# One layer of Mamba and experts in chunks: the residual projection in two buffers, its SiLU beside the gates', the second norm turned earlier

## The reference

```python
def _forward(x, rms_w, W_in, conv_w, conv_b, W_x, W_dt, A_log, W_out):
    xn = _rmsnorm(x, rms_w)
    xs, res = jnp.split(xn @ W_in, 2, axis=-1)
    # xs = silu(causal depthwise convolution of xs with 4 taps + conv_b)
    dt, Bm, Cm = jnp.split(xs @ W_x, [D_INNER, D_INNER + D_STATE], axis=-1)
    dt = jax.nn.softplus(dt @ W_dt)
    # over the tokens: h = exp(A * dt) * h + dt * B * xs;  y = sum over the states of h * C
    y = y * jax.nn.silu(res)
    return x + y @ W_out

x = x + _forward(_layernorm(x), ...)      # x: 1 x 4096 x 256, f32
x = x + experts(_layernorm(x))            # 8 experts, 512 tokens each, width 704:
                                          # (silu(x @ w1) * (x @ w3)) @ w2
```

## Time and profile before

| | |
|---|---|
| median of 3 runs | 1064.31 us (1063.12 to 1065.66) |
| the profiled execution | 1064.04 us |
| its span, first to last instruction | 1062.2 us |
| VectorE busy | 934.8 us, 88% |
| GpSimd busy | 891.4 us, 84% |
| TensorE busy | 944.7 us, 89% |
| ScalarE busy | 698.8 us, 66% |
| mean granted clock of TensorE | 0.958 |

### The profile page before, as it was taken

How to read it: one execution, slowest core, us unless ns; L and a number is a source line. 1 busy time by engine, 2 the same in 40 slices (tenths; PEclk the granted TensorE clock), 3 DMA queues, 4 the chain that set the end, 5 groups by cost and what they waited for, 6 DMA issues and landing times.

```text
span 1062.2 us, 13010 instructions
## 1 busy us (share of the span) xinstructions
PE 944.7 (89%) x4160; PEld 598.6 (56%) x4160; DVE 934.8 (88%) x1011; ACT 698.8 (66%) x1188; POOL 891.4 (84%) x491
## 2 busy tenths in 40 slices
PE   5988789889998999989999889989999897769879
PEld 4554455555664556645665556645666455655655
DVE  5797799899998999898998999898998989998941
ACT  4665675776767766776768867676767766567520
POOL 1598799897998999897998989987998979998910
PEclk9999899999999999989999999999999999769889
DMA  5570153102821047011641029010570026200110
GB/s 162 238 283 20 42 223 134 41 23 94 301 84 62 1 177 300 1 63 55 247 177 39 23 97 356 26 62 1 207 271 6 38 95 257 88 20 6 51 48 20
DMA packets 42852, 117.86 MB, mean 111 GB/s; under 512 B 8608, under 2 KB 27040, under 8 KB 32672
## 3 DMA queue, kind: packets, MB, share of 16 engines
q1 hardware_dynamic: 40928, 116.99, 30.2%
q10 hardware_dynamic: 1856, 0.04, 0.1%
HBM read 110.21 MB, written 6.82 MB: 110 GB/s over the span
## 4 chain that ended last, share of the span: by engine, by line
PE 32%; DVE 31%; issue 15%; ACT 15%; POOL 6%; DMA 1%; DVEq 0%; POOLq 0%; ACTq 0%; SPq 0%
PE gbank L1046 21%; DVE ring L663 20%; DVE ring L648 7%; PE ybank L1109 6%; ACT ebank L801 4%; POOL hc L512 3%; POOL ring L498 2%; PE gbank L1060 2%; ACT sres L865 1%; ACT xs L861 1%; ACT xin L955 1%; ACT L866 1%; ACT hb L985 1%; ACT gbank L916 1%; DVE dt_ L628 1%
## 5 line engine op out<-in xcount | busy, mean ns | idle before, releaser
L663 DVE TENSOR_TENSOR_SCAN ring<-ebank,state,ring 128x512 f32<-128x512 f32 x512 | 624.3, 1268 | 71.5 <-ACT ebank L801 61.5
L512 POOL TENSOR_TENSOR hc<-ring,c_all 128x1024 f32<-128x1024 f32 x255 | 599.1, 2370 | 93.5 <-DVE ring L663 72.0
L801 ACT ACTIVATE ebank<-dt_,a_neg 128x512 f32<-128x512 f32 x512 | 348.4, 688 | 226.3 <-DVE ring L663 223.9
L1109 PEld LDWEIGHTS ybank<-ident,hc 128*128 128x128 f32 x2048 | 241.4, 145 | 139.0 <-issue 77.3
L1109 PE MATMUL ybank<-ident,hc 128*128 128x128 f32 x2048 | 272.0, 281 | 41.9 <-ACT yt L881 26.2
L498 POOL TENSOR_TENSOR ring<-b_all,u 128x1024 f32<-128x1024 f32 x95 | 225.0, 2368 | 0.0
L648 DVE TENSOR_TENSOR ring<-b_all,ubank 128x1024 f32<-128x1024 f32 x159 | 190.2, 1196 | 0.0
L1046 PE MATMUL gbank<-xT,w 128*128 128x512 f32 x320 | 157.1, 631 | 31.4 <-ACT xT L820 18.8
L1046 PE MATMUL gbank<-xT,w_a 128*128 128x512 f32 x256 | 122.8, 620 | 21.2 <-ACT x L948 8.3
L1046 PEld LDWEIGHTS gbank<-xT,w 128*128 128x128 f32 x320 | 60.1, 201 | 93.8 <-issue 78.2
L1046 PE MATMUL gbank<-xs,w_a 128*128 128x512 f32 x224 | 104.2, 609 | 0.0
(11 more groups left out here) (131 smaller groups left out, 750.7 us busy)
## 6 DMA issues: line engine op xcount, KB each, us to landing
b_all<-bc_kept SPq DMA_DIRECT2D x32, 1024.0 KB, 6.8
c_all<-bc_kept SPq DMA_DIRECT2D x32, 1024.0 KB, 8.0
w<-in_L_ffn_w_dram SPq DMA_DIRECT2D x16, 640.0 KB, 4.7
w_a<-wc_kept SPq DMA_DIRECT2D x7, 1024.0 KB, 4.8
w_a<-win_kept SPq DMA_DIRECT2D x6, 1024.0 KB, 5.6
w2s<-in_L_ffn_w_dram SPq DMA_DIRECT2D x8, 640.0 KB, 4.5
xin<-in_L_attn_x_dram SPq DMA_DIRECT2D x9, 512.0 KB, 3.5
x<-in_L_attn_x_dram SPq DMA_DIRECT2D x7, 512.0 KB, 6.8
```

The costliest lines, as they stand in the source:

```text
L512: ch_ok.by(e.tensor_tensor(hc[:, q % HC, :, :], ring[:, q % RING, :, :], c_all[:, n:n + NG, :], ALU.mult))
L663: h_ok.by(e.tensor_tensor_scan(row, ebank[j % 2][:, :], row, initial=state[:, q, n:n + 1], op0=ALU.mult, op1=ALU.add))
L801: e_ok.by(e.activation(ebank[j % 2][:, :], dt_[:, d, :], ACT.Exp, scale=a_neg[:, d, k:k + 1]))
L1109: last = e.matmul(ybank[:, cols(b)], hc[:, q % HC, n, cols(b)], ident[:, :], is_transpose=True, start=(k == 0 and n == 0 and b == 0), stop ...
```

## The change

The buffers `sres_n` and `sres` become `sres[0]` and `sres[1]`, taken by turns by chunk. RES is copied into the buffer of its chunk, its SiLU is done there in place, y is multiplied into it and M reads it. The SiLU is no longer in the block at place 8 but in the gates' block at place 20 (`res_silu`); in iteration 0 the first chunk's stands with the SiLUs of xs and the next chunk's in a block of its own at place 24; iteration 7 has none. GpSimd gets 13 of the 32 B·u products of a chunk, at other tiles. The second norm is applied at place 13 and transposed at 13, ahead of DT 0. Most other jobs move by a place or two, and with PLAN's last numbers the banks change. Left out of the diff: other places where `sres` gets its index, FIRST, and LAST's new place numbers (each engine's order behind the last scan is as before).

```diff
@@ -31,8 +31,8 @@
     AHEAD = 3
     SG = 4
     SQ = SG // NG
-    DVE_BU = tuple(q for q in range(Q) if q % GPD in (0, 2, 4, 6, 7))
-    POOL_BU = tuple(q for q in range(Q) if q not in DVE_BU)
+    POOL_BU = (1, 4, 6, 7, 10, 12, 15, 18, 19, 22, 25, 26, 29)
+    DVE_BU = tuple(q for q in range(Q) if q not in POOL_BU)
     FT = FF // P
     FR = FF - FT * P
     W = 2 * N
@@ -59,8 +59,7 @@
         xs = sb("xs", [P, ND, TC])
         u = sb("u", [P, ND, TC])
         yt = sb("yt", [P, TC])
-        sres_n = sb("sres_n", [P, ND, TC])
-        sres = sb("sres", [P, ND, TC])
+        sres = [sb(f"sres{b}", [P, ND, TC]) for b in range(2)]
...
-        wdt_ld = sres[:, :, :]
+        wdt_ld = sres[1][:, :, :]
...
         PLAN = [
-            (0, "front", "IN", 0, 1.2), (0, "front", "IN", 1, 1.4), (1, "front", "IN", 2, 2.2), (1, "front", "IN", 3, 2.4),
-            (2, "front", "CV", 0, 4.2), (3, "front", "CV", 1, 5.2), (4, "back", "YT", 3, 5.4), (4, "front", "CV", 2, 6.2),
-            (5, "front", "CV", 3, 7.2), (5, "back", "M", 0, 9.6), (5, "back", "M", 1, 9.8), (10, "front", "RES", 0, 11.2),
-            (10, "front", "RES", 1, 11.4), (10, "front", "RES", 2, 12.2), (11, "front", "RES", 3, 12.4), (12, "scan", "YT", 0, 14.4),
-            (12, "front", "BC", 0, 14.2), (13, "front", "DT", 0, 18.3), (14, "back", "OXT", 0, 15.4), (16, "back", "GATE", 0, 17.2),
-            (16, "back", "GATE", 1, 17.4), (17, "back", "GATE", 2, 18.2), (17, "back", "GATE", 3, 18.4), (18, "back", "GATE", 4, 19.2),
-            (18, "back", "TAIL", 0, 23.5), (19, "back", "UP", 0, 21.3), (20, "scan", "YT", 1, 21.5), (20, "back", "UP", 1, 22.2),
-            (21, "back", "UP", 2, 22.4), (21, "back", "UP", 3, 23.2), (22, "back", "UP", 4, 23.4), (23, "front", "DT", 1, 25.3),
-            (24, "front", "DT", 2, 28.2), (24, "back", "DOWN", 0, 29.2), (27, "front", "DT", 3, 32.4), (27, "back", "DOWN", 1, 32.3),
-            (29, "scan y", "YT", 2, 31.4), (30, "next", "XT", 0, 31.6)]
+            (0, "front", "IN", 0, 1.4), (0, "front", "IN", 1, 2.2), (0, "front", "IN", 2, 2.4), (1, "front", "IN", 3, 0.5),
+            (2, "front", "CV", 0, 2.7), (3, "front", "CV", 1, 5.2), (4, "back", "YT", 3, 5.4), (4, "front", "CV", 2, 8.2),
+            (4, "front", "CV", 3, 6.2), (4, "back", "M", 0, 9.3), (5, "back", "M", 1, 10.6), (7, "front", "RES", 0, 11.4),
+            (10, "front", "RES", 1, 11.7), (10, "front", "RES", 2, 12.2), (11, "scan", "YT", 0, 14.9),
+            (12, "front", "RES", 3, 12.4), (12, "front", "BC", 0, 14.2), (13, "back", "OXT", 0, 14.9),
+            (13, "front", "DT", 0, 18.3), (16, "back", "GATE", 0, 17.2), (16, "back", "GATE", 1, 16.5),
+            (16, "back", "GATE", 2, 19.2), (17, "back", "GATE", 3, 18.4), (18, "back", "GATE", 4, 19.7),
+            (18, "back", "TAIL", 0, 23.5), (18, "scan", "YT", 1, 21.5), (18, "back", "UP", 0, 21.3), (20, "back", "UP", 1, 22.2),
+            (21, "back", "UP", 2, 22.4), (22, "back", "UP", 3, 22.7), (23, "front", "DT", 1, 25.3), (24, "back", "UP", 4, 23.4),
+            (24, "front", "DT", 2, 28.2), (24, "back", "DOWN", 0, 29.2), (25, "front", "DT", 3, 32.4),
+            (27, "back", "DOWN", 1, 32.8), (28, "scan y", "YT", 2, 29.9), (30, "next", "XT", 0, 31.6)]
...
-        PLAN += [(28, "ahead y", "YT", 2, 29.4), (29, "ahead", "M", 0, 36.1), (30, "ahead", "M", 1, 36.2)]
+        PLAN += [(26, "ahead", "M", 0, 37.2), (28, "ahead", "M", 1, 33.6), (29, "ahead y", "YT", 2, 29.5)]
...
-            table = [(0, "scan", u_of(ND - 1)), (9, "back", back), (18, "front", u_of(0)), (21, "handed", hand_on),
-                     (22, "next", front), (25, "front", u_of(1)), (28, "front", u_of(2))]
-            table0 = [(5, "late", u_of(1)), (8, "late", u_of(2)), (10, "late", u_of(3)), (21, "handed", hand_on),
-                      (22, "next", front), (26, "front", u_of(0)), (28, "front", u_of(1)), (30, "front", u_of(2))]
+            table = [(2, "scan", u_of(ND - 1)), (8, "back", back), (16, "handed", hand_on), (16, "front", u_of(0)),
+                     (20, "next", front), (29, "front", u_of(1)), (31, "front", u_of(2))]
+            table0 = [(5, "late", u_of(1)), (6, "late", u_of(2)), (10, "late", u_of(3)), (22, "handed", hand_on),
+                      (23, "next", front), (26, "front", u_of(0)), (27, "front", u_of(1)), (31, "front", u_of(2))]
...
-                    read_out(e.tensor_tensor(sres[:, d, :], bank[:, :], sres[:, d, :], ALU.mult), i, "YT", d)
+                    mine = sres[c % 2][:, d, :]
+                    read_out(e.tensor_tensor(mine, bank[:, :], mine, ALU.mult), i, "YT", d)
...
-            table = [(3, "front", convolved(0)), (4, "back", gated(ND - 1)), (4, "front", convolved(1)), (5, "front", convolved(2)),
-                     (6, "front", convolved(3)), (8, "back", m_stats), (13, "scan", gated(0)), (17, "front", dt_of(0)), (20, "next", x_stats),
-                     (20, "scan", gated(1)), (20, "back", hidden(0)), (21, "back", hidden(1)), (21, "back", hidden(2)),
-                     (22, "back", hidden(3)), (22, "back", hidden(4)), (22, "back", hidden_tail), (24, "front", dt_of(1)),
-                     (27, "front", dt_of(2)), (28, "ahead y", gated(2)), (30, "scan y", gated(2)), (31, "front", dt_of(ND - 1))]
-            table0 = [(0, "late", fed), (4, "late", dt_of(1)), (7, "late", dt_of(2)), (9, "late", dt_of(3)), (15, "front", convolved(0)),
-                      (16, "front", convolved(1)), (17, "front", convolved(2)), (18, "front", convolved(3)), (20, "scan", gated(0)),
-                      (20, "next", x_stats), (23, "scan", gated(1)), (25, "front", dt_of(0)), (27, "front", dt_of(1)),
-                      (29, "front", dt_of(2)), (30, "scan", gated(2)), (31, "front", dt_of(ND - 1))]
-            last = [(0, "back", last_c), (1, "back", gated_last), (2, "back", add_rows("M", 0, x1a_ok)),
-                    (2, "back", add_rows("M", 1, x1a_ok)), (3, "back", x1_stats), (4, "back", normal_last),
-                    (5, "back", turned_last), (6, "back", hidden_last), (7, "back", add_last)]
+            table = [(3, "front", convolved(0)), (4, "back", gated(ND - 1)), (4, "front", convolved(1)),
+                     (6, "front", convolved(2)), (6, "front", convolved(3)), (8, "back", m_stats), (14, "scan", gated(0)),
+                     (17, "front", dt_of(0)), (20, "next", x_stats), (20, "scan", gated(1)), (20, "back", hidden(0)),
+                     (20, "back", hidden(1)), (20, "back", hidden_tail), (21, "back", hidden(2)), (22, "back", hidden(3)),
+                     (23, "back", hidden(4)), (24, "front", dt_of(1)), (27, "front", dt_of(2)), (28, "ahead y", gated(2)),
+                     (30, "scan y", gated(2)), (31, "front", dt_of(ND - 1))]
+            table0 = [(0, "late", fed), (2, "late", dt_of(1)), (7, "late", dt_of(2)), (9, "late", dt_of(3)),
+                      (15, "front", convolved(0)), (16, "front", convolved(1)), (17, "front", convolved(2)),
+                      (18, "front", convolved(3)), (19, "next", x_stats), (19, "scan", gated(0)), (22, "scan", gated(1)),
+                      (27, "front", dt_of(0)), (28, "front", dt_of(1)), (28, "front", dt_of(2)), (30, "scan", gated(2)),
+                      (30, "front", dt_of(ND - 1))]
+            last = [(1, "back", last_c), (2, "back", gated_last), (2, "back", add_rows("M", 0, x1a_ok)),
+                    (3, "back", add_rows("M", 1, x1a_ok)), (3, "back", x1_stats), (5, "back", normal_last),
+                    (6, "back", turned_last), (6, "back", hidden_last), (10, "back", add_last)]
...
             def res(*ds):
                 def job(c, i):
-                    sr_ok.wait(e, c - 1)
+                    if has_back(i):
+                        wait_full(e, i, "M", NT // 2 - 1)
                     for d in ds:
-                        move("RES", d, i, sres_n[:, d, :])
-                return job
-
-            def silus(_, i):
-                c = i + 1
-                if has_front(i):
-                    wait_read(e, i, "CV", ND - 1)
-                    halo_ok.by(e.activation(xpre[:, :, 0:HALO], xpre[:, :, TC:TC + HALO], ACT.Copy))
+                        move("RES", d, i, sres[c % 2][:, d, :])
+                return job
+
+            def halo(c, i):
+                wait_read(e, i, "CV", ND - 1)
+                halo_ok.by(e.activation(xpre[:, :, 0:HALO], xpre[:, :, TC:TC + HALO], ACT.Copy))
+
+            def xs_silus(c, i):
+                halo_ok.wait(e, c - 1)
+                for d in range(ND):
+                    xs_ok.by(e.activation(xs[:, d, :], xs[:, d, :], ACT.Silu, bias=cb[:, d:d + 1]))
+
+            def res_silu(c, i):
+                wait_read(e, i, "RES", ND - 1)
+                sr_ok.by(e.activation(sres[c % 2][:, :, :], sres[c % 2][:, :, :], ACT.Silu))
+
+            def silus(c, i):
+                halo(c, i)
                 e.preload_act_table(ACT.Silu)
-                if has_front(i):
-                    halo_ok.wait(e, c - 1)
```

(56 more changed lines are left out.)

23 lines of the change are left out of this document (11 added, 12 removed), and 3 rows, old and new, of the table FIRST.

## The result

The changed kernel takes 1016.02 us (median of 4, 1013.09 to 1017.51) against 1064.99 before: ratio 0.954 (95% interval 0.951 to 0.957), 49 us less. The profiled execution took 1013.09 us with a span of 1011.3 us, 50.9 us less than before.

A forecast was written before the change was run, and what follows sets the result against it. VectorE's scan chain, losing time to ScalarE, was taken as the bound. A repeated chunk's -5.7 was cut to -4.2; six chunks -25.2, chunk 7 -3.5, chunk 0 +0.8 gave -28 from 1064.04: 1036 us, range 1020 to 1060.

The forecast's parts named there:

- the rule: ScalarE's work after tile q is hidden if within VectorE's other work after q-1 and q plus 0.57 us; about 0.7 accuracy.
- Products, -1.2 of VectorE's work: Each repeated chunk: one B·u product moves to GpSimd, -1.20 us on VectorE, +2.37 on GpSimd.
- Tile 9, -3.0: Wait behind place 8's block: SiLU leaves (1.80 us), a B·u product gives 1.20 more cover; 3.39 becomes 0.4.
- Tile 13, -0.9: Second norm's activations move after tile 13, away from two residual reads, so the 0.89 us wait goes.
- Gates' block, 0.9 us of wait left: Block at tile 20 grows by 1.80 us of SiLU; with new VectorE cover, 0.8 to 0.9 us wait replaces 1.32.
- The norm ahead of dt as the cure of the waits at tiles 19 and 20: Earlier transposes end TensorE's 2.92 us wait, removing every second chunk's 1.80 + 0.73; with the gates' block, -1.9 a chunk.
- New waits, +1.0, and GpSimd, +0.3: Per chunk: +0.7 us after tile 18, +0.3 together after tiles 6 and 28, +0.3 for GpSimd with 13 products.
- Taken off for what the rule doesn't see, 1.5: Reserve turning -5.7 into -4.2 us a chunk, for misses up to 0.9 a place and TensorE's nearly full sum.
- Chunk 0: Tile 20's 5.48 us wait changes by -2.45, the SiLU's own block at 24 adds +4.5, products -1.2: +0.8 in all.
- The signs of being right: Chunks 118 to 119 us; expected waits at tiles 9, 13, 19, 21, 25 and for xT; GpSimd idle 4 to 5.
- the half-gain case: Rival: TensorE or GpSimd becomes the bound once waits go; chunk 120.7 us, total 1050 us; chance 0.18.
- the slower case: Rival: TensorE's place 5 waits for ScalarE's residual, delaying CV 0 and M; chunk 126 us, total 1079; chance 0.12.

The follow-up runs named there:

- e4: Kernel before with only the 13 new GpSimd B·u products at their new tiles: 1044.11 us, ratio 0.976 to 0.987 to before.
- e1: Changed kernel with the old 20 VectorE and 12 GpSimd B·u products at their old tiles: 1043.54 us, ratio 0.974 to 0.985 to before.
- e9: Changed kernel with three jobs at old places (second norm's activations 12, second gate product 21, tail's 22): 1032.17 us, ratio 0.966 to 0.973.
- e5: Kernel before with two buffers, the residual's SiLU in the gates' block and chunk 0's blocks as changed: 1068.55 us, ratio 1.001 to 1.006.
- e2: Changed kernel with the residual's SiLU back in the block at place 8: 1021.32 us, ratio 0.955 to 0.965 to before.
- e7: Changed kernel with the second norm's transposes behind DT 0 again (place 14, read at 15): 1017.56 us, ratio 0.954 to 0.959 to before.
- e8: Kernel before with only the second norm's transposes moved ahead of DT 0 (place 13, read at 14): 1066.69 us, ratio 1.000 to 1.004.
- e3: Changed kernel with old B·u products and the SiLU back at place 8, leaving new places and banks: 1045.01 us, ratio 0.976 to 0.986.
- e10: Changed kernel with tile 19's B·u product on VectorE, 12 on GpSimd: 1029.26 us, ratio 0.966 to 0.971 to before.
- e11: Changed kernel with tile 31's B·u product also on GpSimd, 14 there: 1033.81 us, ratio 0.969 to 0.975 to before.
- e12: Changed kernel with chunk 1's residual SiLU in iteration 1's block at place 8, iteration 0's block at place 24 removed: 1014.40 us, ratio 0.952 to 0.957.
- e13: e12 with iteration 0's fourth DT product at place 27 instead of 25: 1016.80 us, ratio 0.952 to 0.956 to before.
- e14: Changed kernel run again unchanged, on the same chip as e13: 1016.98 us, ratio 0.953 to 0.957 to before.

## Why the forecast was too slow

**What bounded the kernel** was read rightly: VectorE's chain, with its waits for ScalarE. What failed is the rest of a chunk's sum: 1.3 us of new waits (+1.0 and +0.3) that came to 0.2, 1.2 us of small waits that it left standing without a word and that went, and 1.5 us taken off the gain for what the rule doesn't see. Together they are nearly all of the 3.9 us between -4.2 and -8.1. The steps one by one, for a chunk:

- *Products, -1.2 of VectorE's work*: right in kind. Together with the cover they give, e4 shows -3.6 and e1 -4.1 (118.8 against 114.7); the forecast has -1.2, and 1.2 under each of the two blocks, which is 3.6. The 0.45 and 0.95 of e1 (tiles 14 and 29) are not in the forecast. This is the largest part of the change.
- *Tile 9, -3.0*: measured 3.39 to 0.46, -2.9.
- *Tile 13, -0.9*: -0.89, and e9 gives the cause: the place of normal2.
- *Gates' block, 0.9 us of wait left*: 0.72. e9 shows that the two products under it carry 1.3 us, as forecast. The SiLU alone gains nothing (e5) and with the products' covers 1.1 us a chunk (e2).
- *The norm ahead of dt as the cure of the waits at tiles 19 and 20*: this reason fell. e7 undoes it for about 0.5 us a chunk, all at tile 19, and TensorE doesn't wait for xT there either. TensorE's waits for xT between 200 and 770 us, before and in e4, say the same from the other side:

```profile
PE gbank L1046 <- ACT xT L820: 14.6, 5, 2.9
```

```profile
PE gbank L1046 <- ACT xT L820: 0.2, 1, 0.2
```

The new products alone (e4) take that wait away, and VectorE still stands at tiles 19 and 20. What stands ahead of these waits at the old places is ScalarE itself waiting for TensorE's gate products: 12.7 us between 200 and 770 us before, 11.6 in e4 and 18.0 in e8, and none at the new places, in the changed kernel, in e3 or in e7. So TensorE is late with the gates there, whether it has waited for xT or not. The new PLAN makes GATE 2 at place 16, not 17; ScalarE reads y at 18, not 19, and the tail at 20, not 19. Which of these jobs it was no run isolates.
- *New waits, +1.0, and GpSimd, +0.3*: here the step failed. None over 0.1 us came after tile 18, 6 or 28 (but for the 0.42 at tile 29 in the one chunk), and for GpSimd the scans waited 0.26 and 0.43 us in two chunks of six. For the place after tile 18 I summed durations: 1.1 for two gates, 0.58 for y, 0.2 for the state copy, 1.9 us. ScalarE's timeline shows their starts, and VectorE's the four scans of tiles 18 and 19:

```profile
341.29 0.19 ACT L810 ACTIVATE state<-ring 128x4 f32<-128x4 f32 x1
341.39 1.06 ACT L825 ACTIVATE hb<-gbank 128x512 f32<-128x512 f32 x2
342.34 0.59 ACT L902 ACTIVATE yt<-ybank 128x512 f32<-128x512 f32 x1
342.82 1.48 ACT L806 ACTIVATE ebank<-dt_,a_neg 128x512 f32<-128x512 f32 x2
```

```profile
341.13 4.98 DVE L664 TENSOR_TENSOR_SCAN ring<-ebank,state,ring 128x512 f32<-128x512 f32 x4
```

From 341.29 to 342.82 it is 1.53 us, because back-to-back instructions overlap by about 0.1 us each. The rule's allowance is 1.17, so 0.36 is left of the 0.7, and the scans lose 0.1 to 0.2 us (4.98 us for four that take 4.81 elsewhere). The rule itself is over by the rest.
- *Taken off for what the rule doesn't see, 1.5*: the error with the largest size, and its sign was wrong. The kernel before had 1.2 us a chunk of small waits that I left where they were: in every second chunk 0.23 at tile 0, 0.60 at tile 3 and 0.25 for y's last block, and in every chunk 0.70 at tile 29, for GpSimd's product. None of them is left in the changed kernel. The 0.23, 0.60 and 0.25 are absent from e8 and e4 too, where the norm or the products alone changed, so it doesn't take the whole change to lose them; why they go no run isolates. The reserve was also meant for TensorE's own sum, "within 5 us of a chunk of 117"; what came of it is the one chunk of slow matmuls, 0.3 us a chunk on the mean.

Sum: -5.7 without the 1.0 and the 0.3 is -7.0; with the 1.2 it is -8.2; measured -8.1. The forecast said -4.2.

*Chunk 0* was right in its parts: tile 20's wait 5.48 became 2.77 (3.0 expected), and 4.39 stand at tile 25 (4.5). Of these 1.48 stood there before, which the forecast's +4.5 leaves out:

```profile
119.18 2.46 DVE L664 TENSOR_TENSOR_SCAN ring<-ebank,state,ring 128x512 f32<-128x512 f32 x2 [2.77 <-ACT ebank L806]
...
139.66 4.81 DVE L664 TENSOR_TENSOR_SCAN ring<-ebank,state,ring 128x512 f32<-128x512 f32 x4 [4.39 <-ACT ebank L806]
```

```profile
134.35 1.28 ACT L878 ACT_TABLE_LOAD   x1
135.65 1.91 ACT L869 ACTIVATE sres<-sres 128x2048 f32<-128x2048 f32 x1
...
138.87 1.30 ACT L806 ACTIVATE ebank<-dt_,a_neg 128x512 f32<-128x512 f32 x2
```

But up to iteration 1's block the total is -0.7, not +0.8: of the other waits (0.7 to 2.4 us, in part for DT and for u's copy) some went and others came, about which the forecast says nothing. In ScalarE's rows the block's loads take 1.28 us and the next activation follows 1.30 us after a load's start. The drain that the Trainium skill's "ScalarE: Activation LUTs" (What ACT_TABLE_LOAD costs) adds does not appear, and the measured term is the one worked out from the rows. *The rest from iteration 6's block on*: -7.7 forecast, -9.6 measured, although chunk 7's scans wait 2.4 us for GpSimd (1.56 and 0.88). Over 2 us in a chunk was a sign of being wrong; it came in this chunk alone.

*The signs of being right.* As forecast are tile 9 (0.46), tile 13 (none), TensorE's wait for xT (none) and tile 25 of chunk 0 (4.39). Not as forecast are the chunk (114.3, not 118 to 119), GpSimd's idle time (0.65 us a chunk, not 4 to 5) and the wait of about 1 us at tile 19 (0.1, or GpSimd's 0.26 and 0.43).

**The rivals.** GpSimd and TensorE did become full, and the half-gain case rested on this, but they do so at 114.3 us, not at 120.7: being level with VectorE costs the scans 0.7 us over 5.8 chunks. In the slower case M 0 at place 5 waits for the residual. It does, but 1.0 us a chunk and not more than 3 (TensorE's waits between 191 and 850 us):

```profile
PE gbank L1084 <- ACT gbank L937: 4.9, 5, 1.0
```

The scans don't feel it; only in iteration 7 do M's statistics wait for it, 0.86 us. e3 has the new places of M and CV and gains 20 us.

## What to carry to other kernels

In a pipeline of queues in order, price a block on one engine by what the other engine has in its own queue beside it. Moving a block without moving covers moves its wait (e5), while two products of 0.6 and 0.7 us put under it were worth 1.3 us a chunk, and four activations moved out of a crowded place 1.0 (e9); and the product moved to another engine was worth three times its own time, because with the new tiles others stand under the blocks (e1). Sum such work by starts, not by durations, and list all the waits of before, the small ones too, before deciding what a change of all places leaves standing; a reserve for the unknown belongs on both sides.

When three engines are level, a change of one product in either direction can cost over 1% (e10, e11, at the tiles tried), and a wait cut out in one chunk can come back as several small ones (e12, e13, in chunk 0).

## What was not expected

Slow matmuls came right behind a wait of TensorE, whatever the wait was for, but not behind every one. Before, six waits of 2.92 or 2.93 us for xT are equal; behind three of them eight matmuls take 5.37, 6.72 and 6.74 us, behind the others 3.67, 3.67 and (seven on record) 3.24, where 3.6 is the normal time. In e8 all six waits of 3.32 us for BC are followed by 5.37. In the changed kernel waits of 1.75 to 1.93 us are followed by full speed and one of 2.10 by 3.38 us for four matmuls at a granted clock of 0.56; in e14 one of 1.87 is followed by 2.48 and one of 2.12 by the normal 1.98. So the length of the wait alone doesn't tell; what else decides it no run here shows. The granted clock of a chunk is 1.00 (the full level, 2.4 GHz), 0.99 in the one with the slow four, where it was 0.97 to 0.99. The Trainium skill's "TensorE: Matmul & The Clock Gate" (Part 1) has the array throttled until activity releases it. The slow stretches behind waits agree with it; the equal waits with 3.67 after them don't show it.

The wait for the first exponential at 48 us was 1.55 us in the first profile of the changed kernel and 4.84 in e14's. It belongs to the start-up, and the 3.3 us between the two are of the size of the spread between executions (1013 to 1018 us). A difference of 2 us between two versions, as in e12, can't be read from one profile's span for that reason.
